# A DLRM tower on one core: SyncE fetches the rows of seven gathers instead of five, and three orders change in the end

## The reference, cut to what matters

```python
e = stack([tbl_f[ids[:, f]] for f in range(26)], axis=1)   # 2048 x 26 x 64, one row of each table per sample
x = layer_norm(dense_t @ Wd.T, gd, bd)                     # 2048 x 128
y = layer_norm(einsum('bnd,ed->bne', e, Ws), gs, bs)       # 2048 x 26 x 128
y = layer_norm(einsum('bne,pn->bep', y, Wsi), gsi, bsi)    # 2048 x 128 x 32
T = concatenate([x[:, None, :], swapaxes(y, 1, 2)], 1)     # 33 vectors of 128 per sample
Z = einsum('bnd,bmd->bnm', T, T)[:, TRIL_I, TRIL_J]        # 528 products per sample
z = layer_norm(Z @ Wl.T, gl, bl)                           # 512, of which 384 are used
h = relu(concatenate([z, dense_t], 1) @ W_top1 + b_top1)   # 512
h = relu(h @ W_top2 + b_top2)                              # 256
out = h @ W_top3                                           # 2048 x 1
```

## Time and profile before

| | |
|---|---|
| time, median of 3 runs | 564.98 us (564.25 to 565.21) |
| the profiled execution: its time | 564.77 us |
| its span, first to last instruction | 563.0 us |
| PE busy | 502.4 us (89%), mean granted clock 0.988 of full |
| POOL busy | 400.4 us (71%) |
| DVE busy | 397.1 us (71%) |
| ACT busy | 291.8 us (52%) |
| DMA engines, queue of POOL | 12.7% of the span |
| DMA engines, queue of SP | 11.4% of the span |

### The profile page before, as it was taken

How to read it: one execution, slowest core, us unless ns; L and a number is a source line. 1 busy time by engine, 2 the same in 40 slices (tenths; PEclk the granted TensorE clock), 3 DMA queues, 4 the chain that set the end, 5 groups by cost and what they waited for, 6 DMA issues and landing times.

```text
span 563.0 us, 20133 instructions
## 1 busy us (share of the span) xinstructions
PE 502.4 (89%) x7271; PEld 376.5 (67%) x7271; DVE 397.1 (71%) x710; ACT 291.8 (52%) x758; POOL 400.4 (71%) x422
## 2 busy tenths in 40 slices
PE   1968869999999999998989999898989999998988
PEld 0844536767676767776666777776667676867666
DVE  4686975877677777767667776777687676668720
ACT  1543565546463654555464555545465555546533
POOL 6777777777777777777777777777777777777310
PEclk9998889999999999999999999999999999999999
DMA  7811221313122221313131131313122131313020
GB/s 237 286 29 28 66 52 29 92 31 93 27 74 47 68 55 29 94 28 93 28 86 36 34 88 28 92 31 93 28 69 52 28 91 31 93 27 84 16 68 2
DMA packets 32222, 36.06 MB, mean 64 GB/s; under 512 B 11945, under 2 KB 21022, under 8 KB 32122
## 3 DMA queue, kind: packets, MB, share of 16 engines
q0 software_dynamic: 13296, 13.71, 12.7%
q1 hardware_dynamic: 18826, 21.05, 11.4%
HBM read 25.54 MB, written 9.18 MB: 62 GB/s over the span
## 4 chain that ended last, share of the span: by engine, by line
POOL 61%; issue 22%; PE 7%; DMA 4%; DVE 4%; ACT 1%; DVEq 0%; ACTq 0%; POOLq 0%
POOL rows L672 61%; DMA rows<-in_table,ids_based 4%; PE bank_z L829 2%; PE bank_z L755 1%; DVE scaled L397 1%; DVE scaled L422 1%; DVE y L435 1%; PE bank_b L788 1%; PE bank_z L808 1%; PE bank_aw L885 1%; PE bank_b L872 1%; DVE r_vec L461 0%; ACT y_std L1050 0%; DMA ids_based<-in_ids_first 0%; DVE bank_z L453 0%
## 5 line engine op out<-in xcount | busy, mean ns | idle before, releaser
L672 POOL DMA_INDIRECT rows<-in_table,ids_based x411 | 394.2, 959 | 127.8 <-issue 122.3
L445 DVE TENSOR_REDUCE y_var<-y_sq 128x32 f32<-128x1024 f32 x61 | 74.4, 1220 | 39.2 <-ACT y_sq L1044 39.0
L1044 ACT ACTIVATE y_sq<-y 128x512 f32<-128x512 f32 x128 | 80.6, 631 | 33.4 <-DVE y L435 32.9
L808 PEld LDWEIGHTS bank_z<-r_vec 128*32 128x32 f32 x4096 | 47.9, 110 | 57.8 <-issue 54.9
L788 PE MATMUL bank_b<-mixed,gs_row 64*128 64x512 f32 x128 | 74.9, 666 | 11.6 <-ACT mixed L1080 9.7
L461 DVE TENSOR_TENSOR r_vec<-y,bank_z 128x512 f32<-128x512 f32 x122 | 78.4, 683 | 2.1
L453 DVE RECIPROCAL bank_z<-y_std 128x32 f32<-128x32 f32 x61 | 22.0, 361 | 77.3 <-ACT y_std L1050 77.3
L1073 ACT ACTIVATE row_std<-row_var,eps 128x8 f32<-128x8 f32 (+1 forms) x64 | 19.2, 300 | 109.0 <-DVE row_var L406 99.5
L829 PE MATMUL bank_z<-wl,zd 128*128 128x512 f32 x160 | 75.2, 615 | 0.1
L788 PE MATMUL bank_c<-mixed,gs_row 64*128 64x512 f32 x128 | 74.9, 666 | 0.0
L761 PE MATMUL bank_z<-gram,rows_t 128*128 128x128 f32 x416 | 64.6, 295 | 9.3 <-ACT rows_t L1065 9.0
(11 more groups left out here) (138 smaller groups left out, 637.3 us busy)
## 6 DMA issues: line engine op xcount, KB each, us to landing
rows<-in_table SPq DMA_DIRECT2D x640, 0.2 KB
zx<-zs SPq DMA_DIRECT2D x15, 560.0 KB
rows<-in_table,ids_based POOLq DMA_INDIRECT x411, 2.5
dense_t<-in_dense_t SPq DMA_DIRECT2D x1, 2048.0 KB, 9.2
wl<-in_wl SPq DMA_DIRECT2D x1, 1280.0 KB, 12.7
w<-in_w SPq DMA_DIRECT2D x1, 1280.0 KB
zd<-zx SPq DMA_DIRECT2D x15, 80.0 KB
zd<-zx SPq DMA_DIRECT2D x15, 70.0 KB
```

The lines of the kernel that those rows point to most:

```text
L445: v.tensor_reduce(y_var[:, k % BANKS, :], y_sq[:, k % 2, :, :].rearrange("e a (s p) -> e (a s) p", p=PROJ), AX_X, ALU.add).then_inc(y_var_ ...
L672: nc.gpsimd.indirect_dma_start(rows[t % ROWS_KEPT][:, c, D * blk:D * (blk + 1)], None, io["table"], bass.IndirectOffsetOnAxis(ap=ids_all[: ...
L808: mm = pe.matmul(bank_i[PROJ * s:PROJ * (s + 1), n * ITEMS:(n + 1) * ITEMS], own[:, Y0:PAD], own, start=True, stop=True)
L1044: nc.scalar.activation(y_sq[:, k % 2, blk, :], y[:, k % 2, blk, :], ACT.Square).then_inc(y_squared, 1)
```

## The change

SP's share grows to seven tiles: OWN_TILES is (3, 5, 7, 9, 11, 13, 15), 896 rows instead of 640, and POOL has 409 gathers instead of 411. One TENSOR_LOAD takes up to sixteen row numbers. The first fetch has 100 rows, an iteration 60, eight of them between zx and the moves; the last rows are asked for in iteration 13. The wait for the buffer now stands right before the group's first row, and no longer before the load of its numbers. In the end of PE third_layer(last - 1) goes ahead of first_layer_last(). In the end of ACT keep_mixed(w + 3) goes ahead of square(w + 2, 0), and y_root_block(w + 3, 1) ahead of keep_z(w + 2).

```diff
-OWN_TILES = (3, 6, 9, 12, 15)
+OWN_TILES = (3, 5, 7, 9, 11, 13, 15)
 OWN_CHUNK, OWN_BLK = CHUNKS - 1, 1
 OWN = P * len(OWN_TILES)
-OWN_FIRST, OWN_PART, OWN_BETWEEN = 44, 44, 4
+OWN_FIRST, OWN_PART, OWN_BETWEEN = 100, 60, 8
+OWN_LOAD = 16
...
                 end = min(end, OWN)
-                for at in range(first, end, 4):
+                for at in range(first, end, OWN_LOAD):
                     if at == 0:
                         sp.wait_ge(own_ready, 1)
-                    if at % P == 0 and OWN_TILES[at // P] >= ROWS_KEPT:
-                        sp.wait_ge(rows_scaled, BANKS * (OWN_TILES[at // P] - ROWS_KEPT + 1))
                     _, numbers = nc.values_load_multi_w_load_instructions(
-                        own_ids[0:1, 1, at:at + 4], engines=(mybir.EngineType.SP,), min_val=0, max_val=io["table"].shape[0] - 1,
+                        own_ids[0:1, 1, at:min(at + OWN_LOAD, end)], engines=(mybir.EngineType.SP,), min_val=0,
+                        max_val=io["table"].shape[0] - 1,
                         skip_runtime_bounds_check_because="a row number of a table of that many rows, by the inputs' kind")
-                    for n in range(4):
+                    for n, number in enumerate(numbers):
                         g, p = divmod(at + n, P)
                         t = OWN_TILES[g]
+                        if p == 0 and t >= ROWS_KEPT:
+                            sp.wait_ge(rows_scaled, BANKS * (t - ROWS_KEPT + 1))
                         sp.dma_start(rows[t % ROWS_KEPT][p:p + 1, OWN_CHUNK, D * OWN_BLK:D * (OWN_BLK + 1)],
-                                     io["table"][bass.DynSlice(numbers[n], 1), :]).then_inc(own_landed[g], 16)
+                                     io["table"][bass.DynSlice(number, 1), :]).then_inc(own_landed[g], 16)
...
                 turn_z(last)
+                third_layer(last - 1)
                 first_layer_last()
-                third_layer(last - 1)
                 second_layer_last()
                 third_layer(last)
...
             y_root(w + 1)
             keep_z(w)
+            keep_mixed(w + 3)
             square(w + 2, 0)
-            keep_mixed(w + 3)
             square(w + 2, 1)
             y_root(w + 2)
             square(w + 3, 0)
             keep_z(w + 1)
             square(w + 3, 1)
             y_root_block(w + 3, 0)
+            y_root_block(w + 3, 1)
             keep_z(w + 2)
-            y_root_block(w + 3, 1)
             keep_z(w + 3)
```

## The result

| | before | after |
|---|---|---|
| time, median | 565.03 us (564.25 to 565.21, 4 runs) | 586.69 us (585.87 to 587.84, 4 runs) |
| ratio after / before, 95% interval | | 1.0379 (1.0361 to 1.0398) |
| span of the profiled execution | 563.0 us | 585.2 us |
| granted TensorE clock, mean | 0.988 | 0.959 |

A forecast was written before the change was run, and what follows sets the result against it. POOL's gathers, 1.25 us each, were taken as the bound, by about 1 us a tile in the second half. Gathers 2.50 plus swaps 0.75 and 0.4 made 3.65 us off, giving 561.3 us; own range 560.2 to 562.4, whole range to 566.

The forecast's parts named there:

- the load of sixteen ... I take it near the lower, 0.6: SP's TENSOR_LOAD of sixteen numbers: priced at 0.6 us, between 0.557 (all fixed) and 2.23 (proportional to four numbers' load).
- The nearest row: Profile row of SP's TENSOR_LOAD of four numbers, 0.557 us, used to price the load of sixteen.
- The 0.46 minimum: Minimum time of SP's four-number load, in us, read as a part waiting and not reading.
- the sum closed exactly at one end: SP's iteration: 29.1 + 2.1 = 31.2 us against 31.2 to 32.4 per tile, if a load of sixteen costs what four cost.
- 0.9 us decided it: SP's loads: from about 0.9 us each, SP would exceed POOL's 32.1 us per tile by over 3.6 us in 13 tiles.
- full but not late: SP's queue: 31.2 us per iteration against 31.2 to 32.4 per tile, slipping some tenths a tile up to tile 6, then recovering.
- SP becomes the bound: Rival at SP's TENSOR_LOAD: proportional cost gives 36.8 us iterations and 626 us; 1.4 us loads give 34.0 and near 585; chance 0.20.
- The free lateness: SP's zx before ScalarE's copy of the next tile's first z part: up to 3.6 us late costs nothing.
- The gathers: POOL has 409 instead of 411; the last starts 2 x 1.25 = 2.50 us earlier and TensorE follows; low end 1.25.
- the second rival: TensorE's own order holds it between 470 and 524; 1.25 or less of 2.50 comes through: 563.0 us; chance 0.13.
- The swaps: End of the kernel: two reorderings on ScalarE give 0.75 us together, the third layer moved on TensorE gives 0.4 net.
- So it passes on: TensorE's last interaction: the 0.75 us from ScalarE's reorderings reaches the last tile's linear through zs, zx and zd.

The follow-up runs named there:

- with 56 rows: The changed kernel with 112 rows first and 56 per iteration: 563.26 us, 0.9960 of before; a second run also carried loads over the calls: 563.84 us, 0.9969.
- the third layer alone: The kernel before with only third_layer of tile 14 moved ahead of first_layer_last on TensorE: ratio 0.9990.
- loads of 28: Seven tiles, three swaps, carried loads, 112 rows first, 56 per iteration, loads of 28 numbers, none right behind zx: 562.59 us, 0.9956 of before.
- six tiles: The changed kernel with OWN_TILES (3, 5, 7, 9, 12, 15), 112 rows first, 48 per iteration, loads of sixteen: 563.64 us, 0.9967 of before.
- the root alone: The kernel before with only y_root_block(w + 3, 1) moved ahead of keep_z(w + 2) on ScalarE: ratio 0.9989.
- the first experiment: The kernel before, SP's old share of five tiles and 44 rows per iteration, with loads of sixteen and no swap: 565.68 us, ratio 1.0001.
- both carried kernels: The changed kernel with loads of sixteen continuing across fetch calls: 563.84 us (0.9969) with 56 rows per iteration, 584.26 us (1.0305) with 60.

## Why the prediction was wrong

**The step that failed** is "the load of sixteen ... I take it near the lower, 0.6". It measured 1.23, between the ends of 0.557 and 2.23. The nearest row was one point, four numbers at 0.557, and I read it as a fixed cost. A load of four is base and one block: 0.33 + 0.22. From the row alone the split could not be known. The 0.46 minimum in that row, on which the prediction leaned, says nothing of it. Since the sum closed exactly at one end, and 0.9 us decided it, the forecast had a margin of 0.3 us on a cost it had not seen. With it failed the wait that hangs on it: SP, taken as full but not late, was 28 us late with the zx of tile 13, and the kernel went at SP's pace and not at POOL's. All three signs of being wrong that the prediction names came: a load over 1 us, a zx late by more than 3.6 us, and last turns that no longer wait for DMA.

**SP's iteration.** Forecast 31.2, measured 34.1. Three loads of sixteen are 3 x 0.67 = 2.0 of the 2.9, the load of eight behind zx at 1.05 another 0.5; single stalls of some tenths are the rest. The other terms held: 0.42 per row, eight rows in 3.16, moves 2.61, no wait for zx left. The first fetch was late by the same cost, ending at 66.75 instead of near 63, and still before the first zx.

**The rival came true.** "SP becomes the bound" had 0.20. Its mechanism is shown by the runs with loads of four (+ 51 us for 3.5 us of iteration) and with 56 rows (- 23 us for 2.2). Its 585 us for an iteration of 34.0 fit the 586.7 for 34.1, in part by luck: it came to 34.0 with a load of 1.4, and for the 1.23 measured the same sum gives an iteration of some 33.4 and a time near 576. The load of eight behind zx and the stalls, which it did not have, make up the rest. The range ended at 566, although the prediction itself left nearly 0.2 beyond it and priced that case at 585 to 626.

**The free lateness** of 3.6 us was right. With 56 rows zx left 2.2 to 5.7 us after ScalarE's fourth copy of the tile. Up to 3.8 us late ScalarE had no wait; in tiles 4 to 12, at 4.9 to 5.7, it waited 0.9 to 1.9 (in the last two of the 15 its next copy comes later, and it had none). In after it waited 11 times, up to 4.1 us.

**The gathers.** The mechanism is borne out: the last turn starts 2.4 to 2.6 us behind the last gather in eight traces (before, loads of sixteen, all three swaps, the third layer alone, both runs with 56 rows, loads of 28, six tiles); with the root alone it was 3.9, and in after, where SP sets the pace, 26.5. And the last gather starts sooner by what was priced: in five traces each, 2.4 us for two gathers fewer (last section). Of the size in time less is settled. Swaps alone 0.09%, with one gather less 0.33%, with two 0.44%: some 1.3 us for the first, 0.6 for the second and 2.0 together, where 1.25 each were forecast. Each ratio has an interval of 0.12 to 0.16% to either side, so the 2.0 is good to some 1.2 us: two gathers fewer gain something, but neither 2.5 nor 1.25 is excluded. Nor is it settled what takes the missing part of the second: SP, which has no room in any run with seven tiles, or TensorE's own order (the second rival, 0.13).

**The swaps**: forecast 0.75 + 0.4. In the profiles 0.79 at the interaction, of which 0 to 0.6 reached the last linear, and 0.3 for the third layer; in time 0.5 us, with an interval from 1.2 less to 0.3 more. The start of the interaction was forecast rightly, 13.7 us behind the last turn against 13.6 measured; "So it passes on" was not, as the way through zx and zd spreads by half a us.

## What to carry to other kernels

An engine that only issues DMAs has a budget like any other: add up its iteration from rows, and where a change fills it to the last tenth, the one price that is not in the trace decides. Before a batch is made four times larger, measure the larger batch with the old load of work (the first experiment here, 1.0001 of the time before), then fill the room that it really gives. And when a run is meant to have room, look whether it does: here the waits of SP for ScalarE's copies tell it, and in every run with seven tiles they were close to nothing while it had rows to fetch. Numbers loaded into registers were cheapest in long runs that begin at a multiple of four and do not stand right behind the 560 KB of zx.

## What the runs showed of the hardware

- A TENSOR_LOAD from SBUF into SP's registers took 0.33 us and 0.22 for each aligned four numbers (0.557 for 4, 0.79 for 8, 1.006 for 12, 1.227 for 16, 1.447 for 20, 1.90 for 28); not aligned to four, or fewer than four, it took 0.33 and 0.20 for each number (0.51 for 1, 0.73 for 2, 1.93 for 8).
- Started 0.4 us behind the issue of a DMA of 560 KB from SBUF the same load was slower: 2.03 to 2.14 us for sixteen, 1.81 and 1.85 for twelve, 1.02 to 1.21 for eight, but 0.50 for four. From twelve numbers on the excess was 0.8 to 0.9 us whatever the size. The DMA's packets ran from 0.86 to some 2.4 us after its issue. That the transfer is what slows the load is argued from this, not shown.
- The mean granted TensorE clock was lower where TensorE was held up more: 0.988 before, 0.959 with SP's iteration at 34.1, 0.922 at 37.6, and 0.988 again with 56 rows. The means are made of stretches at the full clock (2.4 GHz) and short ones at half of it. TensorE's busy time rose from 502.4 us before to 511.8 in after for the same 7271 matmuls. That this cost nothing beside an SP that sets the pace is argued, not shown.
- POOL's last gather started at 521.5, 523.1, 522.4 and twice 523.5 in five profiled executions with 411 gathers, and at 520.6, 520.6, 521.2, 519.7 and 520.0 in five with 409 (after, 56 rows, both carried kernels, loads of 28). The means are 2.4 us apart, but single executions of one kind spread by up to 2 us, as much as two gathers are worth.
